# An adaLN mixer and expert block on one core: the last three modulation rows as column groups of one TensorE pass

## What is computed

```
mod = (silu(c) @ wmod).reshape(4, 6, 1, 512)
sa, ca, ga, sb, cb, gb = mod[:, 0..5]
ga, gb = sign * max(|.|, 0.25)
h = layernorm(x) * (1 + ca) + sa
x = x + ga * mixer(h)
h = layernorm(x) * (1 + cb) + sb
x = x + gb * experts(h)       # argmax of two experts, times its softmax weight
```

## Time and profile before

| | us |
|---|---|
| median of 3 runs | 557.66 (556.89 to 558.77) |
| the profiled execution | 557.73 |
| its span | 555.9 |
| TensorE busy | 509.6 (92%) |
| VectorE busy | 349.3 (63%) |
| ScalarE busy | 264.2 (48%) |
| GpSimd busy | 151.0 (27%) |

### The profile page before, as it was taken

One profiled execution on the slowest core, in us unless ns is written; L12 is line 12 of the kernel. 1 busy time (PEld: TensorE's weight loads), 2 busy tenths in 40 slices (PEclk: granted clock), 3 DMA queues, 4 the chain that ended last, 5 costly groups with the idle time before them and its releaser, 6 DMA issues.

```text
span 555.9 us, 7679 instructions
## 1 busy us (share of the span) xinstructions
PE 509.6 (92%) x2280; PEld 386.9 (70%) x2280; DVE 349.3 (63%) x729; ACT 264.2 (48%) x524; POOL 151.0 (27%) x170
## 2 busy tenths in 40 slices
PE   7899899999188999999999999999999999999960
PEld 1354355535166888898888888889888888878850
DVE  4588999899999575464445454446444545456780
ACT  1763387956786643443442353345344335332310
POOL 1100003121433420330150043033015003734883
PEclk9999999999679999999999999999999999999995
DMA  8920442220150004030022022003002200234995
GB/s 303 425 108 0 152 153 76 77 77 2 25 202 4 4 3 153 17 136 2 1 77 78 1 77 78 1 9 146 2 1 77 78 1 1 86 98 98 156 122 72
DMA packets 15008, 44.19 MB, mean 79 GB/s; under 512 B 5016, under 2 KB 5016, under 8 KB 11624
## 3 DMA queue, kind: packets, MB, share of 16 engines
q1 hardware_dynamic: 10600, 34.71, 17.6%
q0 software_dynamic: 4352, 8.69, 8.9%
HBM read 34.94 MB, written 8.71 MB: 79 GB/s over the span
## 4 chain that ended last, share of the span: by engine, by line
PE 71%; DVE 18%; issue 4%; ACT 3%; POOL 1%; DMA 1%; DVEq 1%; ACTq 0%; SPq 0%; POOLq 0%
PE bank L1086 33%; PE bank L1060 32%; DVE xc L1214 4%; DVE res L1252 2%; DVE st L1259 1%; DMA x_in<-x 1%; PE bank L903 1%; PE bank L944 1%; PE bank L948 1%; DVE st L1196 1%; POOL out L563 1%; DVE eabs L1276 1%; PE bank L917 1%; PE bank L927 1%; ACT XSfull L694 1%
## 5 line engine op out<-in xcount | busy, mean ns | idle before, releaser
L512 POOL TENSOR_TENSOR Wlo<-raw,Whi (+1 forms) x60 | 76.4, 1303 | 232.5 <-ACT Whi L822 227.1
L1520 DVE TENSOR_TENSOR acc<-acc,bank 128x512 f32<-128x512 f32 x119 | 81.0, 687 | 66.8 <-PE bank L1086 61.2
L1060 PE MATMUL bank<-XShi,Whi 128*128 x320 | 116.4, 364 | 7.2 <-DVE XSlo L1486 6.2
L1060 PE MATMUL bank<-XSlo,Whi 128*128 x320 | 115.8, 362 | 0.0
L1060 PE MATMUL bank<-XShi,Wlo 128*128 x320 | 115.7, 361 | 0.0
L1504 DVE TENSOR_TENSOR twice_h<-twice_h,bank 128x512 f32<-128x512 f32 (+2 forms) x80 | 48.2, 606 | 97.2 <-ACT twice_h L807 95.3
L1086 PE MATMUL bank<-Whi,ahi 128*128 128x512 f32 x272 | 106.3, 391 | 3.0 <-DVE alo L1510 1.9
L1086 PE MATMUL bank<-Wlo,ahi 128*128 128x512 f32 x272 | 106.1, 390 | 0.0
L1086 PE MATMUL bank<-Whi,alo 128*128 128x512 f32 x272 | 106.0, 390 | 0.0
L816 ACT ACTIVATE ahi<-twice_h 128x512 fp32r<-128x512 f32 (+2 forms) x80 | 45.4, 568 | 122.9 <-PE bank L1086 114.6
L807 ACT ACTIVATE twice_h<-bank 128x512 f32<-128x512 f32 (+2 forms) x80 | 42.3, 530 | 89.9 <-PE bank L1060 75.0
(11 more groups left out here) (176 smaller groups left out, 532.3 us busy)
## 6 DMA issues: line engine op xcount, KB each, us to landing
raw<-wffn SPq DMA_DIRECT2D x16, 1024.0 KB, 5.2
wm<-wmod SPq DMA_DIRECT2D x6, 1024.0 KB, 12.2
out<-res SPq DMA_DIRECT2D x4, 1024.0 KB, 4.5
x_in<-x SPq DMA_DIRECT2D x3, 1024.0 KB, 12.2
ga_bc<-ga_rows SPq DMA_DIRECT2D x4, 256.0 KB, 3.5
x<-x SPq DMA_DIRECT2D x1, 1024.0 KB, 5.2
bc<-router_rows_scaled SPq DMA_DIRECT2D x4, 256.0 KB, 3.5
wx_sb<-wx SPq DMA_DIRECT2D x1, 514.0 KB, 8.4
```

The lines of the kernel that those rows point to most:

```text
L512: pool.tensor_tensor(Wlo[:, hb % 2, c, :], raw[:, c, :], Whi[:, hb % 2, c, :].bitcast(F32), ALU.subtract).then_inc(s_wlo, 1)
L1060: mm = pe.matmul(hP[(par + u) % 2][m][:, c0:c1], W[wp][:, par, 2 * e + k // 2, o:o + P], XS[xp][:, k, bass.ds(start_row[u] + c0, c1 - c0)] ...
L1520: dve.tensor_tensor(acc[:, n, :], acc[:, n, :], yP[s][:, :], ALU.add).then_inc(s_yu, 1)
```

## The change

The twelve matmuls of rows 3, 4 and 5 are made in one place, in batch 0's turn, by `last_mod_rows`. The loop over the four blocks of the contraction is outermost and the three rows are inside it; row 3 goes to columns 0 to 31 of the array, row 4 to 32 to 63, row 5 to 64 to 95 (`tile_position`), and so to partitions 0, 32 and 64 of the one bank `pT[0]`. Both sets of columns, 3 and 4, now go to `pT[1]`. The two turns stand behind `C_product(1)` instead of around it. ScalarE's copy of row 5 moves from batch 2's turn to just behind `decay(1)`, and the first transposes of batch 2 wait for it instead of for columns 3; the second ones wait for columns 4 as before. VectorE's copy of columns 3 waits until both rows are turned.

```diff
--- before.py
+++ after.py
@@ -375,8 +375,10 @@
         FROM_BACK = ROWS - P
         out_bank = (pO[0], pO[1], pX, pB)
         ORDER = (1, 2, 3, 0)
-        row_bank = (pO[0], pX, pO[0], pT[0], pT[1], pO[1])
-        col_bank = (pO[1], pO[1], pO[1], pT[0], pT[1])
+
+        row_bank = (pO[0], pX, pO[0], pT[0], pT[0], pT[0])
+        row_tile = (0, 0, 0, 0, 32, 64)
+        col_bank = (pO[1], pO[1], pO[1], pT[1], pT[1])
 
         place_bank = [(pT[0], pT[1], pT[0], pT[1])] * (NB - 1) + [(pD, pX, pO[0], pO[1])]
 
@@ -596,7 +598,7 @@
                     act.wait_ge(s_mc, 4)
                     act.wait_ge(s_wdr, 1)
 
-                act.activation(mod_row[r % 2][:, :], row_bank[r][0:NB, :], ACT.Identity,
+                act.activation(mod_row[r % 2][:, :], row_bank[r][row_tile[r]:row_tile[r] + NB, :], ACT.Identity,
                                bias=1.0 if r in (0, 3) else 0.0).then_inc(s_rw[r], 1)
 
             def normalize1(b):
@@ -736,6 +738,7 @@
             mod_row_copy(3)
             mod_row_copy(4)
             decay(1)
+            mod_row_copy(5)
             guess2(0)
             modulate1(2, (0, 1))
             guess1(3)
@@ -767,7 +770,6 @@
             log_part(3)
             place(1, (1, 2, 3))
             decay(3)
-            mod_row_copy(5)
             guess2(2)
             normalize2(2)
             margin_exp(2)
@@ -858,14 +860,22 @@
 
                 if r == 2:
                     pe.wait_ge(s_rw[0], 1)
-                if r in (3, 4):
-                    pe.wait_ge(s_hT, KT * 2)
-                if r == 5:
-                    pe.wait_ge(s_x2, TJ * 2 + 1)
                 for k in range(KT):
                     mm = pe.matmul(row_bank[r][0:NB, :], sc[:, NB * k:NB * k + NB], wm[r][:, k, :],
                                    start=(k == 0), stop=(k == KT - 1))
                 mm.then_inc(s_mm, 1)
+
+            def last_mod_rows():
+                for r in (3, 4, 5):
+                    pe.wait_ge(s_wm[r], 16)
+
+                pe.wait_ge(s_hT, KT * 2)
+                for k in range(KT):
+                    for r in (3, 4, 5):
+                        mm = pe.matmul(row_bank[r][row_tile[r]:row_tile[r] + NB, :], sc[:, NB * k:NB * k + NB], wm[r][:, k, :],
+                                       start=(k == 0), stop=(k == KT - 1), tile_position=(0, row_tile[r]))
+                        if k == KT - 1:
+                            mm.then_inc(s_mm, 1)
 
             def turn(r):
 
@@ -886,9 +896,12 @@
                 for k in ks:
 
                     wait(pe, s_e0, KT * (TJ * (b - 3) + k + 1))
-                    if b == 2 and k < 2:
-
-                        pe.wait_ge(s_cols, 3 + k)
+                    if b == 2 and k == 0:
+
+                        pe.wait_ge(s_rw[5], 1)
+                    if b == 2 and k == 1:
+
+                        pe.wait_ge(s_cols, 4)
                     wait(pe, s_hT, KT * b + k - 1)
                     for j in range(TJ):
                         if k == 0:
@@ -935,8 +948,6 @@
                         pe.wait_ge(s_rw[2], 1)
                 if j == 1:
                     wait(pe, s_x2, TJ * b)
-                    if b == NB - 1:
-                        pe.wait_ge(s_rw[5], 1)
                 if j >= 2:
                     pe.wait_ge(s_bu, b + 1)
                 pe.wait_ge(s_diag, KT * (b + 1))
@@ -1014,15 +1025,14 @@
                     permuted_block(b - 1, 3)
                 if b == 0:
                     delta_product(1)
-                    mod_rows(3)
-                    mod_rows(4)
-                    turn(3)
+                    last_mod_rows()
                 elif nxt:
                     permuted_block(b - 1, 0)
                     permuted_block(b - 1, 1)
                 if nxt:
                     C_product(b + 1)
                 if b == 0:
+                    turn(3)
                     turn(4)
                 if b == 1:
                     transposes1(b + 2, (0, 1))
@@ -1033,8 +1043,6 @@
                 if b > 0 and nxt:
                     permuted_block(b - 1, 2)
                     permuted_block(b - 1, 3)
-                if b == 2:
-                    mod_rows(5)
                 if nxt:
                     state_product(b + 1)
                 if b + 2 < NB:
@@ -1317,7 +1325,8 @@
 
             def mod_columns(r, n):
                 o = KT * NB * (r % 3)
-                dve.wait_ge(s_mc, r + 1)
+
+                dve.wait_ge(s_mc, r + 1 if r < 3 else 5)
                 dve.tensor_copy(cols[:, n, :, :].rearrange("p k b -> p (k b)"), col_bank[r][:, o:o + KT * NB]).then_inc(s_cols, 1)
 
             def assign_first():
```

## The result

| | us, median | range | runs |
|---|---|---|---|
| before | 558.42 | 556.89 to 561.57 | 20 |
| after | 560.88 | 558.53 to 562.61 | 20 |

The ratio is 1.0039, 95% interval 1.0024 to 1.0054: the changed kernel is slower by about 2.2 us, the side of rival 2. The forecast of 557.9 (556.3 to 559.9) and its 0.85 for "within 0.3%" were wrong. The forecast was made against 557.66, the median of three runs, where twenty give 558.42, so 0.8 of the 3.0 us between 557.9 and 560.88 belong to the baseline; the ratios, 1.0004 forecast and 1.0039 measured, leave that out. The profiled execution of the changed kernel took 561.01 us with a span of 559.2, 3.3 us more than that of before.

What follows compares the result with a forecast made beforehand. The prediction took VectorE to bound the mixer stage, so TensorE's savings were hidden: 557.7 - 0 - 0 + 0.2 (late clock fall) = 557.9 us, chance 0.57, range 556.3 to 559.9 us.

Steps and rivals of the forecast that it cites:

- rival 2: Clock falls in both TensorE gaps and comes back late: 1.1 + 0.9 = 2.0 us, 559.7 us, slower; chance 0.12.
- What bounds the stage: Mixer stage, 50 to 150 us: VectorE is the bound, with two waits over 98 us, 0.5 and 0.2 us.
- The block: The twelve matmuls of rows 3 to 5 on TensorE take 5.7 us, ends 3.5 and 10.6; 0 on the path.
- The order's new wait: Batch 2's first transposes wait for ScalarE's copy of row 5, until about 66.0 us; costs nothing.
- The early fall: Clock fall around 64.4 to 68.4 us: if it comes, 0 to 1.1 us reaches VectorE; not in the sum.
- The late fall: Half clock expected after the 4.6 us pause ahead of 130.3 us: 0 to 1.1 us reaches VectorE, 0.2 taken.
- Rivals 1, 3 and 4: Column groups do not overlap, 558.2 us, 0.22; are dearer, 569 us, 0.03; TensorE's saving shows, 554.2 us, 0.06.

Runs made afterwards that it cites:

- fill_both: Changed kernel plus seven spare matmuls, three before batch 2's first transposes and four ahead of state_product(3); 0.9999 of before.
- fill_late: Changed kernel plus four spare matmuls ahead of state_product(3), where row 5 used to be made; 1.0017 of before.
- rows_outer: Changed kernel with the block's two loops exchanged: all four matmuls of row 3, then row 4, then row 5; 1.0025 of before.
- warm3_before: warm2_before plus one spare matmul at 18 us, ahead of batch 0's last transposes; 0.9969 of before, median 556.67 us.
- warm2_before: Kernel before plus spare matmuls in the pauses between mixer and experts and two ahead of the experts' first output products; 0.9987 of before.

## Why the prediction was wrong, point by point

- **What bounds the stage: right.** VectorE waits only 0.7 us between 54 and 152 us in before and 0.7 us in fill_both, so the 7.0 us less TensorE work (3.5 for three rows in place of 7.03 for two and 3.53 for the third) had next to nothing to give back. No run shows this saving by itself: with the pauses filled, 6.2 of the 7.0 us are back, and without, the clock falls.
- **The block: mis-sized.** Predicted 5.7 us, with 3.5 and 10.6 as ends; measured 3.5, the lower end. The argument from the order of instructions was wrong: overlap goes beyond neighbours. The Trainium skill, page "TensorE: Matmul & The Clock Gate", Part 3, has 2.38 for three column tiles; here 10.6 / 3.5 is 3.0 with the rows innermost and 1.5 with them outermost. The mistake bears on the rest through what it made longer: TensorE was done with B_product(1) at 63.1, not 64.4, and the pause behind it was 3.1 us, not 1.6. Whether the clock would have stood a pause of 1.6 us there, no run shows.
- **The order's new wait: right as a place**, 66.1 us and ScalarE's copy of row 5 at 65.5 as computed, **but priced at nothing by itself**; its price is the clock.
- **The early fall: the step that failed first.** The forecast gave it a range of 0 to 1.1 us and then left it out of the sum. It cost 0.9 us. What follows state_product(1) started at 74.1 instead of 72.3, a loss of 1.8 us against the 1.0 us of slack read off: 0.8 is left, and VectorE's new wait is 0.7. The slack was right; the fall had been left out. The trace of before had a row that spoke for it and was not read: behind a pause of only 2.02 us, at 164.7 us, the clock was at its lower level to 168.1 us. "1.00 from the start to 144 us" is right, but the second fall lies behind that.

```profile
164.67 0.78 PE L1060 MATMUL bank<-XShi,Whi 128*128 x1 [2.02 <-DVE XSlo L1486]
```

```profile
166.00:168.00 2.00, 2.00 (x6) 1.52 (x6) 1.78 (x7) 2.00 (x6) 0.00 (x0) 0.50 0.36 147
```

- **The late fall: expected, and mis-sized.** I took 0.2 us out of 0 to 1.1 and it cost 1.2. The first state output starts 3.7 us later (137.34 for 133.66). Of this 1.0 is VectorE's own lateness from the first pause; TensorE loses 2.7: 0.4 on the first matmuls behind the mask (0.87 us to the next start instead of 0.47) and 2.3 on the diagonal ones (5.15 instead of 2.89). That is above the 1.0 to 2.5 given: the work at half the clock took 6.0 us (0.87 + 5.15), where 2 to 5 had been allowed. Less the slack of 1.4 to 2.0, 0.7 to 1.3 follow, and VectorE waited 1.0. That the slack "covers most of the loss" did not follow from the rows: already at 2.5 the same subtraction gives 0.5 to 1.1.
- **Rival 2 was what happened**: it gave 2.0 us, as 1.1 and 0.9, and the difference is 2.2, as 0.9 early and 1.2 late in the profile. Its chance of 0.12 was too low. Both falls came in pauses that the text had itself computed (3.0 us in two pieces, and 4.6 us), so they belonged in the forecast, and the clock that stays up should have been the rival. Its counter-argument, that half of the losses computed lie under the slack, weighed losses of 1.0 to 2.5 us; they were 1.8 and 2.7, both above their slacks of 1.0 and of 1.4 to 2.0.
- **Not in any case: the third place.** A fall at 174.8 us, ahead of the stage where TensorE is the bound, cost about 1 us in the profiled execution; it comes in some profiles with and without either pause, which fits that the profiled difference (3.3 us) is larger than that of the medians (2.2 from the ratio).
- **Rivals 1, 3 and 4 are out**: the groups overlap, are not dearer, and no saving shows.

## What to carry to other kernels

Work that is taken out of a stage in which its engine is not the bound can cost time on TensorE: here the clock fell to half in the holes of 3.1 and 4.8 us and stayed there for what followed. When a sum shows a new pause of a few us on TensorE, price the next work at half speed first, and compare that loss with the slack behind it. Read the trace of before for every fall, also those that cost nothing, and for the pause ahead of each. Fill a hole with spare matmuls where the work behind it is waited for, and leave it where another engine is the bound. Small scatter between executions is worth a look at the granted clock: fifteen spare matmuls took 0.3% off this kernel and nearly all of its spread (4.5 to 0.5 us). Only the whole set was told from 1.000; what the spare matmul at 18 us gave by itself was not run.

## What the hardware showed

- Float32 matmuls with 4 stationary columns in three column groups of one bank ran fully side by side: 24 instructions in 3.54 us, as long as 8 alone, if neighbours are of different groups; with each group's four matmuls in a row, 7.0 us.
- The half clock lasted about 7 us at each of the two new places in the changed kernel (65.5 to 72.4, and 130.4 to 137.2 us by the granted clock of the stretches), and came back while the work went on. The same places had shorter falls in other profiles: 3.4 us in fill_late (67.9 to 71.3, VectorE's wait for the exponential 0.2 us) and in rows_outer (132.1 to 135.6, no wait of VectorE for its residuals), where the long ones cost VectorE 0.7 and 1.0 us. The clock also fell where the late work was only held back in pieces with pauses of up to 1.34 us between them; what exactly decides is left open.
- A short hole of 1.08 us behind transposes and turns at 18 us was enough in the traces of some kernels (the clock 0.50 in 20 to 22 us) and not in those of others with the same code up to there; with one spare matmul of 1.1 us in it the twelve executions of warm3_before spread over 0.5 us instead of the 3.2 of warm2_before (timed on another chip), from which I infer that it no longer fell there; a trace shows that for one of them only.
